# A four-layer kernel: a new interleaving of its streams, and a branch moved inside its products

## The reference, cut to what matters

```python
x = x + _L0_attn_ref(_layernorm(x), ...)   # 16 heads of 8, softmax over 1024 keys, wo, layer norm
x = x + _L0_ffn_ref(_layernorm(x), ...)    # ternary weights, 128 -> 512 -> 512 -> 512 -> 128
x = x + _L1_attn_ref(_layernorm(x), ...)   # gated linear attention, a scan over 1024 tokens
x = x + _L1_ffn_ref(_layernorm(x), ...)    # per sequence 3 of 8 expert zones, 128 -> 512 -> 128

# _L0_ffn_ref, the layer whose products the change touches
h = silu(_tlin(x, w1_w, w1_s)) * _tlin(x, w2_w, w2_s)
h = gelu(_tlin(h, h1_w, h1_s), approximate=False)
h = gelu(_tlin(h, h2_w, h2_s), approximate=False)
return _tlin(h, w3_w, w3_s)               # _tlin(x, w, s) = (x @ w.T) * s

# _L1_attn_ref, per head with 16 keys and 16 values
h = h * exp(g_t)[..., None] + k_t[..., None] * v_t[..., None, :]     # one step per token
o_t = einsum('bhk,bhkv->bhv', q_t, h)                                # then rms norm, gate, Wo
```

## Time and profile before

| | us |
|---|---|
| median of 3 runs (lowest, highest) | 1151.24 (1147.3, 1154.31) |
| the profiled execution's own time | 1147.3 |
| its span, first to last instruction | 1145.4 |
| mean granted clock of TensorE | 0.961 of full speed |
| PE busy | 1023.5 |
| DVE busy | 675.7 |
| ACT busy | 834.1 |
| POOL busy | 405.9 |

### The profile page before, as it was taken

How to read it: one execution, slowest core, us unless ns; L and a number is a source line. 1 busy time by engine, 2 the same in 40 slices (tenths; PEclk the granted TensorE clock), 3 DMA queues, 4 the chain that set the end, 5 groups by cost and what they waited for, 6 DMA issues and landing times.

```text
span 1145.4 us, 16807 instructions
## 1 busy us (share of the span) xinstructions
PE 1023.5 (89%) x5970; PEld 500.8 (44%) x5970; DVE 675.7 (59%) x1227; ACT 834.1 (73%) x1073; POOL 405.9 (35%) x391
## 2 busy tenths in 40 slices
PE   2799999999999999999696888879697889989898
PEld 1232333333333333333483555646364345656568
DVE  3122444445263434314656988999899899998210
ACT  2699999999999999998466657676674675643541
POOL 1000010101010000100433797788868876967100
PEclk8799999999999999999798999989897899999999
DMA  5765553626363544500000000000001121010110
GB/s 125 119 119 108 102 102 76 122 56 125 67 106 78 114 70 84 98 19 14 20 1 28 28 2 28 1 28 1 29 1 41 43 63 51 16 48 27 28 47 19
DMA packets 101456, 64.59 MB, mean 56 GB/s; under 512 B 62388, under 2 KB 91860, under 8 KB 99284
## 3 DMA queue, kind: packets, MB, share of 16 engines
q1 hardware_dynamic: 101328, 62.98, 26.6%
q10 hardware_dynamic: 24, 0.25, 0.1%
HBM read 45.10 MB, written 17.83 MB: 55 GB/s over the span
## 4 chain that ended last, share of the span: by engine, by line
PE 58%; DVE 18%; ACT 9%; POOL 6%; issue 5%; SPq 2%; DMA 2%; DVEq 0%; ACTq 0%; POOLq 0%
PE PS L1447 26%; PE PS L1432 15%; DVE R L1250 6%; PE PS L1482 4%; PE PS L1617 4%; PE PS L1606 3%; DVE R L1241 3%; POOL R L865 2%; DVE RB L1197 2%; PE PS L1376 1%; POOL RB L839 1%; PE PS L1362 1%; PE PS L1544 1%; DVE R L1203 1%; DVE R L1207 1%
## 5 line engine op out<-in xcount | busy, mean ns | idle before, releaser
L902 ACT ACTIVATE R<-PS 128x1024 f32<-128x1024 f32 x512 | 474.4, 1088 | 59.2 <-PE PS L1432 58.5
L1447 PE MATMUL PS<-R 128*32 128x512 f32 x2048 | 314.1, 608 | 1.2 <-issue 1.2
L865 POOL TENSOR_TENSOR R<-R 128x512 f32<-128x512 f32 x128 | 187.1, 1466 | 64.3 <-DVE R L1250 59.2
L1432 PE MATMUL PS<-RA 34*128 34x512 f32 x1024 | 189.5, 448 | 20.0 <-DMA RA<-QD 19.4
L1482 PE MATMUL PS<-RB,WR 128*128 128x512 f32 x640 | 183.6, 432 | 22.1 <-DVE R L1203 11.0
L1250 DVE TENSOR_TENSOR_SCAN R<-R 128x512 f32<-128x512 f32 x128 | 200.7, 1569 | 0.0
L1432 PEld LDWEIGHTS PS<-RA 34*128 34x128 f32 x1024 | 77.2, 186 | 216.3 <-issue 193.7
L1482 PEld LDWEIGHTS PS<-RB,WR 128*128 128x128 f32 x640 | 123.8, 197 | 66.8 <-DVE R L1203 12.8
L1447 PEld LDWEIGHTS PS<-R 128*32 128x32 f32 x2048 | 68.2, 108 | 105.8 <-issue 94.0
L829 POOL PARTITION_ALL_REDUCE R<-R x8 | 3.0, 374 | 287.7 <-DVE R L1089 287.7
L839 POOL TENSOR_TENSOR RB<-R,RB 128x512 fp32r<-128x512 f32 x48 | 77.7, 1623 | 55.4 <-ACT RB L912 46.6
(11 more groups left out here) (139 smaller groups left out, 1139.8 us busy)
## 6 DMA issues: line engine op xcount, KB each, us to landing
RA<-QD SPq DMA_DIRECT2D x256, 64.0 KB
QD<-RA SPq DMA_DIRECT2D x128, 64.0 KB, 2.2
RA<-QD SPq DMA_DIRECT2D x64, 128.0 KB
OD<-R SPq DMA_DIRECT2D x128, 32.0 KB, 2.0
R<-OD SPq DMA_DIRECT2D x128, 32.0 KB
VD<-R SPq DMA_DIRECT2D x24, 128.0 KB, 1.8
R<-VD SPq DMA_DIRECT2D x96, 32.0 KB
WP<-in_Wa SPq DMA_DIRECT2D x12, 256.0 KB, 3.2
```

The lines of the kernel that those rows point to most:

```text
L865: pool.tensor_tensor(st, st, Qc[b % 2], ALU.mult).then_inc(S["qh"], 1)
L902: act.activation(PR[u % 4], bank(2 * s, 1024), ACT.Exp, scale=SC).then_inc(S["exp"], 1)
L1432: op = pe.matmul(bank(2 * s + h), exact(KS[k][p:p + 34, gg, 128 * j:128 * j + 128]), exact(QS[k][p:p + 34, gg, :]), start=True, stop=True)
L1447: op = pe.matmul(bank(ob)[c:c + 32, :], VAF[b % 2][:, at:at + 32], PR[u % 4][:, 512 * h:512 * h + 512], start=(j == 0), stop=(j == 7), til ...
```

## The change

Two things change. The test of the flag in `products` moves from behind the first matmul of a sum to ahead of the last one, and behind the wait of that last one. And ORDER is another string with the same letters, each as often as before; it differs from the sixth letter on. One line of it stands here for all ten:

```diff
-    "abcbbccbbccbbbcacbbbbcbbbbacbbbbbbcbbcacbcbacccpbcccbcbcpppcbpcbcpppbcpppcpbbppspsssssscsbcsscsbcbcs"
+    "abcbbbbcbbcabbcbbbbcbabbbcbbcbbcbbccbbccacbccacbcccpbbccpbppbpcpccbpcppbppcpbpsppssssssbscscbcsbspcp"
...
@@ -1481,17 +1481,16 @@
                     l, r = (x, w) if flip else (w, x)
                     return pe.matmul(out_ap, l, r, **kw)
                 seq = [(i, k) for i in range(2) for k in range(len(terms))]
-                for n, (i, k) in enumerate(seq):
+                for n, (i, k) in enumerate(seq[:-1]):
                     w, x, ev = terms[k]
                     need.wait_ge(*ev[i])
-                    op = mm(w(0), x(i), start=(n == 0), stop=(n == len(seq) - 1))
-                    if n == 0:
-                        with pe.If_eq(ternary, 1):
-                            inner = need.inner()
-                            for i2, k2 in seq:
-                                inner.wait_ge(*terms[k2][2][i2])
-                                mm(terms[k2][0](1), terms[k2][1](i2), start=False, stop=False)
-                return op
+                    mm(w(0), x(i), start=(n == 0), stop=False)
+                i, k = seq[-1]
+                need.wait_ge(*terms[k][2][i])
+                with pe.If_eq(ternary, 1):
+                    for i2, k2 in seq:
+                        mm(terms[k2][0](1), terms[k2][1](i2), start=False, stop=False)
+                return mm(terms[k][0](0), terms[k][1](i), start=False, stop=True)
 
             def wpart(n, c0, c1):
                 return lambda j: WR[:, j, n, c0:c1]
```

More of the change, by code:

```diff
@@ L23 @@
 ORDER = (
-    "abcbbccbbccbbbcacbbbbcbbbbacbbbbbbcbbcacbcbacccpbcccbcbcpppcbpcbcpppbcpppcpbbppspsssssscsbcsscsbcbcs"
-    "scsbpspssbpsbcpsbbpsscpbpbsbsbsspssbpbsbsbssspsbssssbpsbcsscsscssbsscspspscpbsccssscbcsssscbscspbpcs"
-    "sssbbcpsspcssspcpspsbspssbcsssbctpccppbbpsbpsscsptsstssbsttctssbbtbsstbsscssbbcsstbcbssbstbbstcsbbbp"
-    "sbscptssccspbcppsctssbsctbspssspcsbsssbsssspsbtcsppbscbscpbscsscbttspstsccsttcstbbcpbsscctpbcstcssts"
-    "ssppctbsscscsbssbsbstsspbcspsbscsssptsstbsbssbscsppbtcscpstssbssccsstscpppcppssctcsspcbtssctsbbpsspb"
-    "tcsscccpssscsssttccsstsbtpstcstscstscscsssccsststcscctspstbscssttsbpsspsspsscssssspssbpspsppssscstpp"
-    "sssscspspzsststdsstttsspzdtdzsttssssdtssdtssssdpsssdtdstststpsdsssdspssdstssssspsstsdpdsspspptpdtsts"
-    "pssspstdzszsssppstsssptssdztsssttssststsdttdsssdsstpdsdstdsssstssstpsssspsddsspsssspsstpsdsppsspptss"
-    "tsssttsdsststsstdssddsstdssssdtsstsssssdsstssdstdsssdtttssssstssdtststzstszssdsttsdstsststztdddsssts"
-    "tssstdssssdtsdssdssssstttssssdsssdssttttdtttddttdttdtdttdtttttzdzddddddzddtddddddddddddddddd"
+    "abcbbbbcbbcabbcbbbbcbabbbcbbcbbcbbccbbccacbccacbcccpbbccpbppbpcpccbpcppbppcpbpsppssssssbscscbcsbspcp"
+    "bsscssbbbpcbpbpscbscbbspcscssbbbbsscbsbcssbsbsssssbcppcpsccsccpsssspbssspsbsspsscbbspcpspsccsbbspsbc"
+    "sccsbpssscpbbpssccsppcssbbpbsbbppcbpssssbcssscbssspbsscbtsbcssbsbcpbctstbsssbssstcttbctcssbctssbcttc"
+    "sscccsssbsssbssssbspsptbpsbccsbtbscsbscpsbsbsccssctbpcbscssbtbssbsbscsssppssbsbssscbppctpscppsttsssb"
+    "sscstssttbbttsbscpccssccpsbtbtccbstcpscpbsbpctssctpsccscstssspcstsssccpspssptspccbpspspsstsssbpcccts"
+    "cssptssstsccptsscbpssspctssstsscsssstsscststczzzstdsdpsstssdtsptsstsddssdpssstsspsdptsssssssdsssstpp"
+    "ppsspsspsstpspsptsstsspssdsstsstttsttsdstsssdtsddtssssdssssptstdspsptstssspssstpppsspptsstpsssptzpsd"
+    "pststtzssstdtzssstsssdtsssdttdsstsssdstsstsdsdssptssstsdsssssspsspsssdpspsdsspssdssssdspspsptspspsst"
+    "tsssssststtdsdsstsdsttssstssdtdtsssdstsstsststsssstsdtdssstssszsdsdssszsdsstsstsdzssdsstsstsddssssss"
+    "ttsdtsstssstsdsststsdstsssstddtdtsssssttttttdttdtdddtttttdttttdtzdtzddzddddddddddddddddddddd"
 )
```

## The result

The changed kernel takes 1221.6 us (median of 4 runs, 1220.1 to 1231.46) against 1151.08 in the same comparison: ratio 1.063, 95% interval 1.057 to 1.068. The forecast was 1156 with a range of 1143 to 1170. The profiled span is 1221.7 us, 76.3 more than before.

The account below looks back on a forecast made before the run. DVE was taken to set the pace between the scans, PE at start and end. The terms 8.2 - 1.5 + 0 - 1.9 = +4.8 us gave 1152.1 against the profiled execution, 1156 against the median, range 1143 to 1170.

Parts of the forecast that it names:

- Between the scans: nothing: First to last scan: both orders have about the same distances, so no change; bounds -15 and +10 us.
- The start: about 8.2 us later: Ahead of the first scan: PE stalls and denser work delay the scan's first product 8.2 us; bounds 3 and 11.
- The chunk: Start: residual(7)'s chunk on DVE delays a low part that hid_mm(6,0,0)'s last matmul needs; price 4.4 us.
- The norm: Start: POOL's norm now precedes block 0's low part, m = 3, which hid_mm(2,0,0)'s last matmul awaits; price 1.3 us.
- the terms of 1.9 and 0.6 us: Start: two gate_mm fall into PE's dense stretch, 1.9 us; hid_mm(6,0,0) waits for the fourth gelu, 0.6 us.
- The way of v: Start, from v's projection to its last part: 6.2 us instead of 7.7, so 1.5 us come back.
- the projection of k: Start: it now stands behind the replica's wait, making the first product 1.5 us later.
- The test of the flag: 1.5 us less: Sums in products: testing ahead of the last matmul removes PE's issue waits, 1.5 us less; bounds 0 and 3.9.
- Behind the last scan: 1.9 us less: Last scan to end: earlier tanh and output product, partly offset by zone weight waits, 1.9 us less; bounds -4, +1.
- DVE's idle time: Rival between the scans: idle time shrinks as ternary blocks finish earlier; half gone, 12.6 us, gives 1143; chance 0.27.
- The contention: Rival between the scans: DVE and POOL hinder each other more, stretching scans by 12 us, giving 1168; chance 0.18.
- The start's delay: Rival at the start: the delay does not reach the scan, giving 1149; chance 0.05.

Follow-up runs that it names:

- e13: Changed kernel, second half of every ternary sum rereading the high part, so no sum waits for a low part (output not the reference's): 1164.6 us, ratio 1.009.
- e14: Old order with new products, sums rereading the high part so that none waits for a low part: 1149.6 us, ratio 0.997.
- e6: New order up to the first scan step, old behind it, with residual(7) moved two letters later and project(7) one: 1164.0 us, ratio 1.010.
- e1: Changed kernel with the old ORDER put back, keeping the new products (moved test): 1154.1 us, ratio 1.002 to the kernel before.
- e2: Changed kernel with the old products put back (test behind the first matmul), keeping the new ORDER: 1219.1 us, ratio 1.056.
- e15: Changed kernel with the first matmul repeated in 16 sums to fill PE's idle waits, 44 us of extra matmuls: 1211.7 us, ratio 1.049.
- e8: Old order with new products, every ternary step opening a level moved up directly behind its stream's previous step: 1220.0 us, ratio 1.059.
- e10: Old order with new products, only the six down steps moved up directly behind their stream's previous step: 1191.0 us, ratio 1.030.
- e7: Old order to the first scan step, new behind; opening sums put off until 3.5 us of DVE work stand between: 1203.9 us, ratio 1.045.
- e9: As e7, but with 7 us instead of 3.5 of DVE work ahead of each down: 1203.3 us, ratio 1.044.
- e11: Old order with new products, opening sums put off to at least 3.5 us of DVE work, downs to 7: 1175.1 us, ratio 1.018.
- e12: As e9, but with 5.5 us of DVE work ahead of opening sums and 8 ahead of downs: 1221.1 us, ratio 1.059.

## Why the prediction was wrong, step by step

- **"Between the scans: nothing"** is the step that failed: 0 with bounds of -15 and +10, measured +52.9. I had counted the steps between a product on PE and the DVE step that needs it, and found them alike. I had not counted the other half of the way, from DVE's low part to the sum that waits for it, which is under 2 us of DVE work at 12 of 23 openings now. The two halves together are a loop, and in the place shown it closes because neither engine has other work queued between. e13 and e14 show that the waits for low parts carry 52 of the 67 us of both stretches. My limit for being wrong, 8 us of idle time, was passed by 43. I also misread a row: the 13.4 us of waits for gelus are of the whole span, and of the 25.2 us between the scans only 4.3 are such waits. The sign of the forecast came out right, and that is no merit: the largest part of the loss has no term in the sum.
- **"The start: about 8.2 us later"** was right in kind and a third of the size: +25.9. The chunk was priced at 4.4 and measured 4.30. The norm was priced at 1.3, a mere shift, and measured a stall of 5.17: `project(7)` on DVE began at 567.19 and not at 563.5. Of these 3.7 us about 1.2 were there before the stretch (PE's first matmul at 556.40 against 555.15). The rest are two waits of 1.27 us (561.42 and 564.25) for ACT's tanh, which stands behind a copy (line 912) that itself waits for DVE's gated value before: another loop, between DVE and ACT. I had moved durations and no waits. e6 shows 9.2 us for this letter. And I set the half clock behind a stall into a bound of 3 us. From the stall at 572.89 to the projection of v PE needs 50.3 us, where it needed 31.4 before; waits of 4.30 and 2.20 us are in it, and the clock is 0.83 from 592 to 623 us, where it was 1.00 from 567.5 to 599. No run measures the terms of 1.9 and 0.6 us by themselves. The way of v gave back 0.7 us instead of 1.5 (24.2 late at its projection, 23.5 at the replica), and the projection of k behind the replica cost 2.4 instead of 1.5.
- **"The test of the flag: 1.5 us less"**: e1 gives +1.6 us with an interval from -1.2 to +5.1, so nothing or a small loss. The `issue` waits were forecast under 6 and are 73.5, because the waits for data are now shown there (e1 and e2 above); how much the test itself costs cannot be read from them. Together with the hand-over it costs little behind such a wait: the low part on POOL ends at 572.59 (571.33 + 1.26) and the matmul starts 0.30 us later.
- **"Behind the last scan: 1.9 us less"**: 2.5 us less (88.5 and 91.0 from the start of the last scan). This held in every kernel with the new order behind the scans but e15. The first wait for the zone's weights was counted as 1.2 us and is 1.11. The second was counted as 1.7; what is there is a wait of 0.72 us, put down to ACT.
- **The rivals**: DVE's idle time did not shrink. The contention had the price of 12 us; in the changed kernel the scans' mean is 1596 ns for 1569, 128 x 0.027 = 3.5 us. In e13 the scans take 10.9 us more than in e14, near the price. The Trainium skill (SBUF — State Buffer, SBUF: two separate sides) has it as an exclusive lock on a port pair, in which the instruction that starts second waits. By that rule the stretching follows the interleaving, and e13 and e14, equal in work and different in order, agree with their 210.8 and 199.9 us. The start's delay did reach the scan. None of the rivals was the one that happened: a wait that appears in both directions at once.

## What to carry to other kernels

When an order is changed in a kernel whose engines feed each other, follow each loop all the way round, from an engine back to itself, and ask how much other work each engine has queued inside it (this rule is drawn from the runs, none tests it alone). A distance on one engine told what closing it costs (e8, e10), and not what opening it gives (e7, e9, e11, e12). Durations that are moved without their waits give the kind of an effect and not its size. Where hand counting has more than a few dozen places, replay the queues with measured durations: here that found a version that beats both, by 0.9% over the kernel before.

## What the runs showed of the hardware

- After the stalls of 3.80 and 4.30 us shown above, PE's ternary matmuls of 512 columns follow each other at 0.43 us instead of 0.23 for some microseconds (7 in 3.21 us from 589.21), and those of 128 columns at 0.22 instead of 0.115 (25 in 5.59 us; before the change 32 in 3.68 us from 584.40). e15 gets back 11.0 of the 52.9 us between the scans by useless work alone.
- Adding 44 us of matmuls to an engine that others wait for can make a kernel faster (1221.6 to 1211.7).
- The same 128 scans on DVE take 199.9 us in one order of the work (e14) and 210.8 in another (e13). Those beside less than 0.2 us of POOL's work take 1.21 to 1.28 us in e13; the longest of all takes 2.31.
- With a branch between a wait for data and the matmul, the profile shows the wait as `issue`: 73.5 us in the changed kernel, where e2, with the same order and the branch elsewhere, has 12.1 and 56.4 for the data.
